# Moving the rows of a relative shift between SBUF tiles: rows 36 partitions apart in place of 32

## The reference

```python
q, k, v = heads(w @ Wq.T), heads(w @ Wk.T), heads(w @ Wv.T)      # (B, H, Lq, 16)
rp = (r @ Wr.T).reshape(2 * Lq - 1, H, d_head).transpose(1, 0, 2)
AC = jnp.einsum('bhid,bhjd->bhij', q + u_bias[None, :, None, :], k)
BD = jnp.einsum('bhid,hjd->bhij', q + v_bias[None, :, None, :], rp)
BD = _rel_shift(BD)                                   # (B, H, Lq, 2 Lq - 1) -> (B, H, Lq, Lq)
attn = jax.nn.softmax((AC + BD) * scale, axis=-1)
out = jnp.einsum('bhij,bhjd->bhid', attn, v)

def _rel_shift(x):
    B, H, Lq, Lr = x.shape
    xp = jnp.concatenate([jnp.zeros((B, H, Lq, 1), x.dtype), x], axis=-1)
    xp = xp.reshape(B, H, Lr + 1, Lq)
    return xp[:, :, 1:].reshape(B, H, Lq, Lr)[..., Lr - Lq:]
```

## Time and profile before

| | |
|---|---|
| median of the runs | 3833.55 us |
| the profiled execution's own time | 3816.15 us |
| its span | 3814.3 us |
| TensorE busy, mean granted clock | 3139.2 us (82%), 0.899 |
| ACT, DVE, POOL busy | 2553.6, 2489.7, 2399.5 us |
| DMA, mean over the span | 180 GB/s |
| moves: issues, size | 4096, 128 KB |

### The profile page before, as it was taken

How to read it: one execution, slowest core, us unless ns; L and a number is a source line. 1 busy time by engine, 2 the same in 40 slices (tenths; PEclk the granted TensorE clock), 3 DMA queues, 4 the chain that set the end, 5 groups by cost and what they waited for, 6 DMA issues and landing times. The chain is left out here.

```text
span 3814.3 us, 115093 instructions
## 1 busy us (share of the span) xinstructions
PE 3139.2 (82%) x40768; PEld 2161.6 (57%) x40768; DVE 2489.7 (65%) x4784; ACT 2553.6 (67%) x3598; POOL 2399.5 (63%) x4232
## 2 busy tenths in 40 slices
PE   4564588889989888988888887888898989889955
PEld 2443266566656566655666665666665666656644
DVE  1544277677767666776767676776676767667845
ACT  2342477777777777776777776777777777777731
POOL 3234577677767666776777676766777667777700
PEclk7787599999999999998999998999999999999977
DMA  8224899898989898888898998988998888999731
GB/s 235 94 87 141 162 197 196 185 188 195 201 186 199 186 190 190 199 189 175 193 193 197 188 195 175 196 192 190 197 199 194 189 191 203 194 182 200 187 118 44
DMA packets 473330, 688.07 MB, mean 180 GB/s; under 512 B 296752, under 2 KB 394928, under 8 KB 404144
## 3 DMA queue, kind: packets, MB, share of 16 engines
q0 software_dynamic: 327680, 537.92, 66.0%
q1 hardware_dynamic: 145072, 142.63, 15.0%
HBM read 90.06 MB, written 52.43 MB: 37 GB/s over the span
## 5 line engine op out<-in xcount | busy, mean ns | idle before, releaser
L630 POOL DMA_DIRECT2D score<-to_move x4096 | 2267.9, 562 | 987.2 <-issue 500.0
L868 ACT COPY to_move<-pos_bank 128x512 f32<-128x512 f32 x2048 | 1108.6, 594 | 660.6 <-PE pos_bank L736 361.6
L928 DVE CUSTOM_DVE_ANT_0 score<-ac_bank,score 128x1024 f32<-128x1024 f32 x512 | 627.1, 1225 | 908.4 <-PE ac_bank L791 875.9
L805 PEld LDWEIGHTS pt_bank<-ident_sb,score 128*128 128x128 f32 x8192 | 1011.8, 146 | 261.6 <-issue 78.2
L805 PE MATMUL pt_bank<-ident_sb,score 128*128 128x128 f32 x8192 | 1121.8, 282 | 39.9 <-issue 31.7
L880 ACT ACTIVATE score<-score,low 128x2048 f32<-128x2048 f32 x512 | 1032.4, 2016 | 33.6 <-issue 23.6
L937 DVE COPY prob_t<-pt_bank 128x512 f32<-128x512 f32 x1536 | 1009.0, 684 | 15.8 <-PE pt_bank L805 15.2
L736 PE MATMUL pos_bank<-pos,qv 96*32 96x512 bf16 (+15 forms) x12160 | 739.2, 327 | 287.8 <-ACT to_move L868 199.9
L928 DVE CUSTOM_DVE_ANT_0 score<-ac_bank,score,low 128x1024 f32<-128x1024 f32 x512 | 656.5, 1282 | 115.0 <-PE ac_bank L791 102.1
L822 PE MATMUL acc_bank<-prob_t,vs 128*32 128x128 f32 x16384 | 692.3, 287 | 20.3 <-issue 20.1
L791 PE MATMUL ac_bank<-ks,qu 96*128 96x512 bf16 x2048 | 650.9, 401 | 27.8 <-issue 17.1
(11 more groups left out here) (94 smaller groups left out, 962.4 us busy)
## 6 DMA issues: line engine op xcount, KB each, us to landing
score<-to_move POOLq DMA_DIRECT2D x4096, 128.0 KB, 6.0
pos<-pos_parts SPq DMA_DIRECT2D x192, 128.0 KB, 10.2
pos_parts<-part SPq DMA_DIRECT2D x32, 384.0 KB, 4.2
ks<-k_parts SPq DMA_DIRECT2D x192, 64.0 KB, 4.7
qu<-qu_parts SPq DMA_DIRECT2D x768, 16.0 KB, 7.8
qv<-qv_parts SPq DMA_DIRECT2D x576, 16.5 KB, 5.3
v_heads<-v_sb SPq DMA_DIRECT2D x8, 1024.0 KB, 7.3
vs<-v_heads SPq DMA_DIRECT2D x32, 256.0 KB, 9.5
```

The costliest lines, as they stand in the source:

```text
L630: pool.dma_start(score[s::QUAD, dst:dst + FT, :], to_move[s::QUAD, src:src + FT, QUAD - 1 - s:QUAD - 1 - s + L])\
L805: last = pe.matmul(PT[(k * NK + c) % 3][:, t * P:(t + 1) * P], lhsT=score[:, slot(k), c * BANK + t * P:c * BANK + (t + 1) * P], rhs=ident_ ...
L868: act.copy(to_move[:, k % (SRC * FT), c * BANK:(c + 1) * BANK], ring(k, c)[:, :]).then_inc(pos_out, 1)
L928: dve.tensor_tensor_reduce(cols, AC[:, :], cols, SCALE, low[:, slot(k), h - 1:h] if h else -NEG, ALU.add, ALU.min, low[:, slot(k), h:h + 1 ...
```

## The change

Each 32-row block is now shifted by four columns more than the block before it, so rows with the same residual shift lie 36 partitions apart. Residual shifts now go from 0 to 43. 20 of them have four rows, eight have three, eight have two and eight have one. The 36 transfers of two to four rows are issued by GpSimd, in an order of its own; the eight of one row are issued by SP, behind the load of `qv` (`move_ends`), and counted on semaphores of their own, for which ACT's `take` and DVE's `add` wait too. The tails are 44 columns wide. `pos` has 16 zeroed columns on either side, since a block's read can now pass its ends.

```diff
@@ constants of the attention stage
             QUAD = 32
-            MWIN = L + QUAD
-            CLUSTER = 4
-            MOVE_ORDER = [CLUSTER * c + i for i in range(CLUSTER) for c in range(QUAD // CLUSTER)]
+            LEAN = 4
+            STRIDE = QUAD + LEAN
+            SHIFTS = QUAD + 3 * LEAN
+            MWIN = L + SHIFTS
+            TAIL = SHIFTS
+            PAD = 16
+
+            def rows_of(shift):
+
+                first = [r for r in range(4) if LEAN * r <= shift < QUAD + LEAN * r]
+                at = QUAD - 1 - shift + STRIDE * first[0]
+                return slice(at, at + STRIDE * (len(first) - 1) + 1, STRIDE), len(first)
+            PAIRED = [QUAD - 1 - 4 * c for c in (0, 2, 4)] + [LEAN + 3, QUAD + 2 * LEAN - 1]
+            OTHERS = [QUAD - 1 - 4 * c for c in (1, 3)] + [2 * LEAN + 3, QUAD + LEAN - 1]
+            ENDS = [LEAN - 1, SHIFTS - 1]
+            MOVE_ORDER = [shift - i for i in range(LEAN) for shift in PAIRED + OTHERS]
+            END_ORDER = [shift - i for i in range(LEAN) for shift in ENDS]
...
-            pos = [s2(f"pos{u}", [STACK, NPOS], BF16) for u in range(2)]
+            pos = [s2(f"pos{u}", [STACK, PAD + NPOS + PAD], BF16) for u in range(2)]
@@ gpsimd
+                for u in range(2):
+                    pool.memset(pos[u][:, 0:PAD], 0.0).then_inc(padded, 1)
+                    pool.memset(pos[u][:, PAD + NPOS:], 0.0).then_inc(padded, 1)
+
                 def move(step, j):
...
-                    for s in MOVE_ORDER:
-                        pool.dma_start(score[s::QUAD, dst:dst + FT, :],
-                                       to_move[s::QUAD, src:src + FT, QUAD - 1 - s:QUAD - 1 - s + L])\
+                    for shift in MOVE_ORDER:
+                        rows, _ = rows_of(shift)
+                        pool.dma_start(score[rows, dst:dst + FT, :], to_move[rows, src:src + FT, shift:shift + L])\
                             .then_inc(moved[j % DST], 16)
@@ sync
+                def move_ends(step, j):
+
+                    wait_apart(sp, pos_out, group(step, j) * ITEMS + ITEMS)
+                    if there(step, FT * (j - DST)):
+                        wait_apart(sp, turned, tile(step, FT * (j - DST + 1)) * NK)
+                    src, dst = j % SRC * FT, j % DST * FT
+                    for shift in END_ORDER:
+                        rows, _ = rows_of(shift)
+                        sp.dma_start(score[rows, dst:dst + FT, :], to_move[rows, src:src + FT, shift:shift + L])\
+                            .then_inc(ends_moved[j % DST], 16)
...
                         load_qv(step, j)
+                    j = (k + POS_AHEAD - 3) // FT
+                    if k % FT == 0 and group_there(step, j):
+                        move_ends(step, j)
@@ tensor
-                        split = min(max((i + 1) * P - moves - first, 0), width)
-                        at = (NI - 1 - i) * P + moves + first
+                        at = (NI - 1 - i) * P + moves + first - LEAN * (row // QUAD)
+                        split = min(max(L - at, 0), width)
...
-                                                 rhs=pos[u][:, at + lo:at + hi], start=True, stop=True)
+                                                 rhs=pos[u][:, PAD + at + lo:PAD + at + hi], start=True, stop=True)
...
-                        last = quads(ring(k, NK), f * QUAD, step, k - FT + 1 + f, L, QUAD)
+                        last = quads(ring(k, NK), f * TAIL, step, k - FT + 1 + f, L, TAIL)
...
+                pe.wait_ge(padded, 4)
@@ scalar, take (the same two waits stand in vector, add)
-                        act.wait_ge(moved[(j - SRC) % DST], use_of_dst(step, j - SRC) * (16 * QUAD) + 16 * QUAD)
+                        act.wait_ge(moved[(j - SRC) % DST], use_of_dst(step, j - SRC) * MOVES + MOVES)
+                        act.wait_ge(ends_moved[(j - SRC) % DST],
+                                    use_of_dst(step, j - SRC) * ENDS_MOVED + ENDS_MOVED)
```

More of the change, by code:

```diff
@@ L525, in build_program @@
             QUAD = 32
-            MWIN = L + QUAD
-            CLUSTER = 4
-            MOVE_ORDER = [CLUSTER * c + i for i in range(CLUSTER) for c in range(QUAD // CLUSTER)]
+            LEAN = 4
[13 more added lines that the diff above has]
+            END_ORDER = [shift - i for i in range(LEAN) for shift in ENDS]
+            assert sorted(MOVE_ORDER + END_ORDER) == list(range(SHIFTS))
             FT = 4
@@ L566, in build_program @@
             moved = [sem(f"moved{i}") for i in range(DST)]
+            ends_moved = [sem(f"ends_moved{i}") for i in range(DST)]
+            padded = sem("padded")
             pos_full, pos_out = sem("pos_full"), sem("pos_out")
@@ L573, in build_program @@
             NLOAD = 16 * len(Q_PARTS)
+            MOVES, ENDS_MOVED = 16 * len(MOVE_ORDER), 16 * len(END_ORDER)
             def tile_steps(eng, body, past):
@@ L642, in _, with load_stacked @@
             def _(sp):
-                def load_stacked(dst, src, order, hd, lo, n, loaded):
+                def load_stacked(dst, src, order, hd, lo, n, loaded, at=0):
                     for i, part in enumerate(order):
-                        sp.dma_start(dst[i * DH:(i + 1) * DH, 0:n],
+                        sp.dma_start(dst[i * DH:(i + 1) * DH, at:at + n],
                                      src[part, bass.ds(hd * DH, DH), lo:lo + n]).then_inc(loaded, 16)
@@ L661, in load_pos @@
                 def load_pos(step, h):
-                    load_stacked(pos[h % 2], pos_parts, K_PARTS, head(step, h), 0, NPOS, pos_loaded[h % 2])
+                    load_stacked(pos[h % 2], pos_parts, K_PARTS, head(step, h), 0, NPOS, pos_loaded[h % 2], PAD)
                 def load_vs(step, h):
@@ L719, in _ @@
                     load_qv(0, j)
+                    move_ends(0, j - 2)
                 tile_steps(sp, body, 4)
@@ L874, in take_tails @@
                     act.copy(to_move[:, j % SRC * FT:j % SRC * FT + FT, L:MWIN],
-                             ring(k, NK)[:, 0:FT * QUAD].rearrange("p (f w) -> p f w", w=QUAD)).then_inc(pos_out, 1)
+                             ring(k, NK)[:, 0:FT * TAIL].rearrange("p (f w) -> p f w", w=TAIL)).then_inc(pos_out, 1)
                 def exponential(step, k):
@@ L922, in add @@
                     if h == 0 and k % FT == 0:
-                        dve.wait_ge(moved[k // FT % DST], use_of_dst(step, k // FT) * (16 * QUAD) + 16 * QUAD)
+                        dve.wait_ge(moved[k // FT % DST], use_of_dst(step, k // FT) * MOVES + MOVES)
+                        dve.wait_ge(ends_moved[k // FT % DST], use_of_dst(step, k // FT) * ENDS_MOVED + ENDS_MOVED)
                     if h:
```

## The result

| | before | after |
|---|---|---|
| median of the runs, side by side | 3830.11 us | 3968.89 us (3962.15 to 3993.72) |
| ratio | | 1.037, 95% interval 1.032 to 1.042 |
| span of the profiled execution | 3814.3 us | 3991.9 us |

What follows compares the result with a forecast made beforehand. Taken as bound: TensorE's 21.9 us floor, with waits for late moves stretching the period to 25.27. Period 22.0 + 0.7 = 22.7 saves 319 us, the start 12, from 3816.15: 3485; plus 17.4 gives 3500 us, range 3400 to 3670.

Steps and rivals of the forecast that it cites:

- Rate of the moves: Moves' DMA queue: rate per engine nearly doubles from 13.4 GB/s, share falls from 66% towards 35%.
- the rival: Moves within SBUF: 13.4 GB/s is the price of such a copy, stride brings nothing; 3970 us, chance 0.06.
- The forecast landing of 3.5 us: Moves: time from a group's last issue to its last landing, 3.5 us, ends 1.5 and 6.0.
- POOL's issues: POOL's queue: 36 issues for 32 take 19.9 us instead of 17.7, still within 21.9 us.
- The chain: Tails to ACT's take two groups on: landing at 23.6 (odd) and 25.2 us (even) against 23.8.
- the lateness: Landing against ACT's take: odd groups just free, even ones 1.4 us late, averaging 0.7 us per group.
- SyncE's eight transfers "hidden": SP's queue: 23.5 transfers per group, 14 us at 0.6 each; loads behind wait 5 us, hidden.
- TensorE: TensorE and ACT: wider tails and more split matmuls add 0.1 us per group, floor 22.0.
- The start: Start of the attention stage: ACT's take of group 2 at 429.7, 6.8 us earlier; 12 us gained in all.
- the one-row transfers crowd few engines: DMA engines carrying SP's one-row transfers: sum 23 to 25.6 us, period 24, 3670 us; chance 0.17.
- The stride doesn't help: Moves within SBUF: same engine time, chain up to 2.2 us longer, period up to 26.4, 3970 us; chance 0.06.
- Slower by SP's queue: SP's queue stays clogged: landing 35.7 us after the tails, deciding from 31.5; period 27.35, 4090 us; chance 0.05.

Runs made afterwards that it cites:

- e1: The changed kernel without its eight one-row transfers and the waits for them, score cleared once at the start: 3767 us, ratio to before 0.989.
- e11: e1 with the pos loads left out from the third head on: 3603 us, ratio to before 0.936.
- e4: The kernel before with the last two of its 32 transfers per group left out: 3799 us, ratio to before 0.995.
- e18: The changed kernel with one-row transfers cut to 64 bytes of each row and tile, issued behind the qv and qu loads: 3829 us, ratio to before 0.997.
- e19b: The kernel before with the six ks loads issued ahead of the qu loads once per head: 3873 us, ratio to before 1.013.
- e17: e1 with, in effect, the six ks loads issued ahead of qu once per head: 3716 us, ratio to before 0.969.

## Why the prediction was wrong, by its steps

1. **Rate of the moves: failed.** "I take nearly the double" was 8%: 14.4 GB/s per engine for 13.4, and 221 for 204 GB/s with engines full. The step took one fact (two engines share a place) for the only limit. The earlier trace rows was a hint in my own reading: 250 GB/s at 0.94 was above that limit (with loads in the mixture), and I used it only to doubt the rival. The Trainium skill (SBUF — State Buffer, Door 1: The DMA port swizzle) says that partitions 32 apart share a port; the doubling was my inference from it. The traces have most of it for the first packets after an idle time (0.68 to 0.46 us) and little of it once the engines are full (0.593 to 0.513 us), and the measurement decides. The forecast landing of 3.5 us was 4.8 to 8.6 by group in e1, and 5.5 to 13.4 in after.
2. **POOL's issues: right.** 19.99 us for 36, and the same price for one to four rows.
3. **The chain: form right, one term missing.** The last issue came at 20.2 and 21.7 us, as worked out, with even and odd groups exchanged. Even and odd groups are coupled, though: the landing of one sets the take of the group two on, which sets the tails that the next one waits for. So a single late group in four, that beside `pos`, costs two periods, and averaging the lateness over equal groups (0.7 us) was the wrong sum. e11 puts 164 us on it.
4. **SyncE's eight transfers "hidden": failed, and it is this step that turned the sign.** Issues took 0.77 us in the median, not 0.6, eight of them 5.58 and 11.96 us in the stretch shown; the loads behind them moved not 5 but 7 to 12 us, into the end of the moves; and TensorE waited 96 us for `qu`. That wait shows in one group of a head, number 1 mod 4: from its first take to its tails pass 24.7 us, in e1 21.0. All four groups of a head together need 3.9 us more for this than in e1, and 10.5 more from tails to the take two groups on, where the landings are. I priced the delay by when the loads are used and not by what they run into. And the bytes themselves, which had no price in this step, cost 71 us by their form. Cost with all its parts: e1 to after, 202 us.
5. **TensorE: too small to be seen.** In the stage its busy time rose from 2838.7 to 2862.1 us, 0.18 a group, but the granted clock fell from 0.93 to 0.90; in e1, with the same wider tails and 0.94, it is 2811.9, under before.
6. **The start: sign wrong.** 448.22 in place of 429.7; before had 436.47. e1 shows what is left of the gain that the step had in mind, some 2 us.

The rivals: *the one-row transfers crowd few engines* had the mechanism right, and its engines named. Its own term was too dear (9.8 us a group, where 32 packets of 0.65 us on four engines are 5.2) and the rest too cheap (9.2 to 12 us at the doubled rate, measured 17.0), so its sum of 23 to 25.6 us held the measured 25.0 by luck; and it took this sum for the period, which a chain of waits sets at 26.6. *The stride doesn't help* (3970) gave the measured time to 1 us, by luck: its chain has no one-row transfers in it, and without these the kernel is faster than before. It had 0.06, and what failed was that both rivals could hold together: little gain from the stride was also what made crowding dear. *Slower by SP's queue* named the queue; its point, a landing 31.5 us behind the tails, was not reached by these transfers (24 us in the mean), but by the moves beside the loads that they had pushed back.

In figures: e4 to e1, the stride with its six more issues, -32 us; tiny transfers +126, of which e18 gives back 65; their bytes as such +5; their bytes in one-row transfers +71; together +170 over e4, which itself lies 26 us under before for its two missing transfers.

## What to carry to other kernels

A transfer added to a queue costs what it pushes back: ask not only when the loads behind it are needed, but what they will run beside. A one-row transfer from SyncE was carried by four engines here, and with the DMA near full the slowest engine sets the landing; so price such bytes by these engines, and the landing by the chain of waits. And when a rate is to double because one shared place goes, look first how much of the gain is left with all engines full: here it was 8%.

## What the runs showed of the hardware beyond that

- GpSimd's queue pauses for some 1.4 us once in two groups, 64 issues apart in before and 72 in after, at the start of an even group there and behind the twentieth issue of an odd one here; what it does then is not known.
- SyncE takes at least 0.567 us to issue a one-row transfer of four pieces, where a load of `qv` took 0.310.
- The span reacts by 44 to 51 us to the exchange of two loads that go out once in a hundred microseconds (e19b, e17).
